# Weight casts and their checks moved from the first to the last groups of an attention stage; the raw weights stay in SBUF

## Chip, cores and metric

The kernel runs on one core of a Trainium2 chip, in one launch. The metric is the device time of that launch in microseconds (us); a run's figure is the median of its executions.

## What is computed

Four sublayers on x of shape (16, 512, 128), each of the form x = x + layernorm(f(layernorm(x))):

```python
x = x + ln(L0_attn(ln(x)))   # 16 heads of 8, keys in 8 blocks of 64, a running maximum
x = x + ln(L0_ffn(ln(x)))    # ternary weights, hidden size 512
x = x + ln(L1_attn(ln(x)))   # FFT of heads, cumulative sum, inverse FFT
x = x + ln(L1_ffn(ln(x)))    # shared expert + top-1 of 8 experts

def L0_ffn(x):
    h = silu(x @ w1.T * s1) * (x @ w2.T * s2)
    h = gelu(h @ h1.T * s_h1)
    h = gelu(h @ h2.T * s_h2)
    return h @ w3.T * s3
```

The change touches the first attention and the first MLP (L0_ffn). The weights w1, w2 (512 x 128), h1, h2 (512 x 512) and w3 (128 x 512) hold -1, 0 or 1.

## The kernel before

The program is a row of blocks, each with one hand-written stream per engine: PE (matmuls), ACT (activations, copies out of PSUM), DVE (reductions, elementwise), POOL (elementwise on SBUF), SP (all ordinary DMAs). Semaphores order them.

**The attention block** works on 16 chunks (one batch row of 512 tokens each) of 4 head groups: 64 groups g = 4 b + i. A step of the pipeline does for group g the scores and their block maxima, for g-1 the differences of maxima, for g-2 the transposed scores, exponentials and products with V, for g-3 the outputs, for g-4 the denominators. PE runs 16 scores (`score`, L568), 16 transposed scores (`score_T`, L579) and 16 products (`pv`, L589) in a step, with one use of PSUM bank 7 per quarter (`bank7`). DVE reduces each of the 16 score tiles out of PSUM (`tile_reduce`, L827), then `previous_max` (L835) ends its step; three PSUM banks rotate between PE and DVE. ACT does 16 exponentials (L678). POOL does the small work on maxima and, per chunk, three normalisations: `normed` (L775) on xnB, on y3 (then `add_residual`, L791) and on xn2. SP loads QR and KR of a group (8 DMAs of 64 KB, L479 and L481) a step ahead, two rows of maxima (`load_max`, L488), and stores q and k of a later chunk (L508, L515). `run_groups` writes steps 0 to 11 out, loops over chunks 3 to 13, and writes steps 56 to 70 out. From step 64 on no scores are left (64 groups), and DVE has only denominators, normalisations and layernorm statistics.

**Weights for the MLP.** The MLP multiplies in a rounded 32-bit type (F32R). Eleven tiles of 128 x 512 (NWB = 11: w1, w2, four of h1, four of h2, w3) are prepared inside the attention block, one per step in steps 0 to 10: SP loads tile n into one of three buffers `w_raw` (`load_weights`, L530), POOL casts it to `wb` (`cast_weights`, L796), and a step later DVE compares raw and cast (`check_weights`: L879 `not_equal` into `w_diff`, L882 `max` into `rounded`), behind `previous_max` of steps 1 to 11.

**The MLP block** starts by reducing `rounded` (L1215) to one number, and PE takes one of two written-out paths: the first multiplies with `wb` (no weight was changed by the cast), the second with 32-bit weights in buffers of its own (w1, w2, hw, w3). SP loads those five buffers (2816 KB in five DMAs, L1008 to L1012) in every run; only the second path waits for them. The trace names `wb` in all MLP matmuls (L1024): the first path runs.

## Time and profile before

| | |
|---|---|
| median of 3 runs | 1799.72 us (1798.75 to 1801.79) |
| the profiled execution's own time | 1799.19 us |
| its span, first to last instruction | 1797.3 us |
| attention block, scores of groups 0 to 63 | 46.4 to 847.7 us |
| its tail, steps 64 to 70 | 847.7 to 895.7 us |
| MLP block begins | 896 us |
| busy over the span: PE / DVE / ACT / POOL | 88% / 74% / 64% / 40% |
| mean granted clock of PE | 0.942 of full speed |

Times in the rows further down are us from the span's start unless marked ns. An arrow at a row's end names what ended the idle time before it. "PEclk" is the granted clock as a share of 2.4 GHz (0.50 is 1.2 GHz). A block of rows with one line number in it is one helper; the names left of the arrow "<-" are what is written, right of it what is read.

### The profile page before, as it was taken

To read this page: it belongs to the slowest core of one execution; us is meant where nothing else is said; L and a number is where in the kernel's file an instruction comes from. 1 tells how busy PE (TensorE), PEld (TensorE's weight loads), DVE (VectorE), ACT (ScalarE), POOL (GpSimd) and SP (SyncE) were. 2 spreads that over 40 slices of the span, in tenths; PEclk is the share of its full clock that TensorE was granted. 3 is DMA by queue.
4 is the path that set the end of the run, shared out by engine and by line. 5 is a ranking of instruction groups with operands and counts; after the bars stand their busy time and mean duration, and the time that the engine had idled before them with its cause. 6 is when DMAs were issued, how large, how long until landed. Compare 5 with 4: busy or idle time off the path is not lost. (4 is left out here: it accounts for less than half of the span.)

```text
span 1797.3 us, 35515 instructions
## 1 busy us (share of the span) xinstructions
PE 1580.2 (88%) x8576; PEld 870.8 (48%) x8577; DVE 1324.0 (74%) x3585; ACT 1146.9 (64%) x2294; POOL 713.0 (40%) x1011
## 2 busy tenths in 40 slices
PE   2899999999999999999499999999498973799996
PEld 1333333333333333333277777777345552566664
DVE  2899999999999999998257666666347763466665
ACT  1387888888888888888466666666236553344342
POOL 2223344344443333322413333333135776144444
PEclk8699999999999999999799999999799985899998
DMA  3333332232323233221010000000120112222210
GB/s 110 75 96 100 86 95 79 81 89 77 93 80 87 79 93 95 72 55 31 13 65 1 1 0 0 0 0 1 27 71 16 44 48 97 72 59 59 59 55 17
DMA packets 84446, 102.48 MB, mean 57 GB/s; under 512 B 15995, under 2 KB 49537, under 8 KB 84368
## 3 DMA queue, kind: packets, MB, share of 16 engines
q1 hardware_dynamic: 78992, 88.89, 17.6%
q0 software_dynamic: 5376, 12.66, 2.0%
q8 instruction: 35, 0.57, 0.1%
q14 instruction: 43, 0.35, 0.1%
HBM read 61.44 MB, written 35.33 MB: 54 GB/s over the span
## 5 line engine op out<-in xcount | busy, mean ns | idle before, releaser
L827 DVE TENSOR_REDUCE bmax<-PS 128x8 f32<-128x512 f32 x1024 | 651.3, 683 | 61.4 <-PE PS L568 58.8
L678 ACT ACTIVATE EX<-PS 128x512 f32<-128x512 f32 x1024 | 565.2, 604 | 107.5 <-PE PS L579 97.9
L568 PE MATMUL PS<-KR,QR 33*128 33x512 f32 x1024 | 411.2, 469 | 50.4 <-DVE bmax L827 31.3
L579 PE MATMUL PS<-QR,KR 64*128 64x512 f32 x1024 | 399.1, 460 | 1.6 <-ACT EX L678 1.5
L568 PEld LDWEIGHTS PS<-KR,QR 33*128 33x128 f32 x1024 | 167.0, 188 | 366.6 <-DVE bmax L827 299.3
L589 PE MATMUL PS<-EX,VS 128*9 128x512 f32 x2048 | 268.6, 596 | 1.2 <-ACT EX L678 1.2
L579 PEld LDWEIGHTS PS<-QR,KR 64*128 64x128 f32 x1024 | 162.5, 185 | 11.3 <-ACT EX L678 10.2
L1024 PE MATMUL PS<-pA,wb 128*128 128x512 f32 x640 | 157.0, 401 | 0.0
L763 POOL TENSOR_TENSOR m_diff<-m_prev,m_all 128x16 f32<-128x16 f32 x64 | 14.2, 222 | 328.1 <-DVE m_all L839 328.1
L1853 ACT ACTIVATE g<-PS 128x512 f32<-128x512 f32 x72 | 43.0, 597 | 142.1 <-PE PS L1813 142.1
L1024 PEld LDWEIGHTS PS<-pA,wb 128*128 128x128 f32 x640 | 120.3, 191 | 27.5
L1170 ACT ACTIVATE gelud<-PS,scales 128x512 f32<-128x512 f32 x128 | 88.3, 690 | 61.5 <-PE PS L1024 58.4
L1124 POOL CAST pA<-gated 128x512 fp32r<-128x512 f32 x64 | 57.6, 899 | 168.3 <-DVE gated L1224 167.9
L1024 PE MATMUL PS<-pB,wb 128*128 128x512 f32 x512 | 120.8, 395 | 0.0
L1024 PEld LDWEIGHTS PS<-pB,wb 128*128 128x128 f32 x512 | 96.1, 188 | 23.4
L1867 POOL TENSOR_TENSOR rs<-ve,neg_half 128x1 f32<-128x1 f32 x72 | 40.8, 566 | 131.8 <-DVE ve L1908 131.8
L1024 PE MATMUL PS<-pX,wb 128*128 128x512 f32 x256 | 75.8, 437 | 19.1 <-DVE gated L1224 16.6
L1224 DVE SCALAR_TENSOR_TENSOR gated<-PS,scales,sil 128x512 f32<-128x512 f32 x64 | 47.1, 747 | 48.2 <-ACT sil L1150 40.8
L1873 POOL DMA_INDIRECT out<-o,idx x72 | 74.4, 1033 | 17.2 <-issue 17.2
L1812 PE MATMUL PS<-sgu,xT 128*128 128x512 f32 x144 | 77.7, 621 | 0.1
L1150 ACT ACTIVATE sil<-PS,scales 128x512 f32<-128x512 f32 x64 | 43.1, 687 | 49.9 <-PE PS L1024 48.8
L1813 PE MATMUL PS<-wgu,xT 128*128 x144 | 74.4, 599 | 0.0
(227 smaller groups left out, 2821.0 us busy)
## 6 DMA issues: line engine op xcount, KB each, us to landing
QR<-q_scr SPq DMA_DIRECT2D x256, 64.0 KB, 2.4
KR<-k_scr SPq DMA_DIRECT2D x256, 64.0 KB, 2.3
k_scr<-partsB SPq DMA_DIRECT2D x42, 256.0 KB, 2.9
rows<-row_scr SPq DMA_DIRECT2D x72, 129.0 KB, 2.1
q_scr<-partsB SPq DMA_DIRECT2D x28, 256.0 KB, 3.0
X<-in_L_attn_x SPq DMA_DIRECT2D x16, 256.0 KB, 3.0
X<-x SPq DMA_DIRECT2D x16, 256.0 KB, 2.4
xB<-in_L_attn_x SPq DMA_DIRECT2D x14, 256.0 KB, 3.3
```

Source lines behind the costliest of these rows:

```text
L568: pe.matmul(PS[:, bank_of(i, n), :], QR[rows, i, h // 2, t * P:(t + 1) * P], KR[rows, i, h // 2, :], start=True, stop=True).then_inc(tile_ ...
L579: pe.matmul(PS[:, RING3 + bank_of(j, n), :], KR[rows, j, h // 2, kt * P:(kt + 1) * P], QR[rows, j, h // 2, :], start=True, stop=True).then ...
L589: mm = pe.matmul(PS[32 * h:32 * h + HD + 1, 6, :], VS[:, j, kt, h, :], EX[:, kt % 2 * HG + head_T(h), :], start=(kt == 0), stop=(kt == NT ...
L678: act.activation(EX[:, n % (2 * HG), :], PS[:, RING3 + bank_of(j, n), :], ACT.Exp, scale=SCALE).then_inc(ex_set, 1)
L827: dve.tensor_reduce(bmax[:, i % 2, n, :], PS[:, bank_of(i, n), :].rearrange("p (b k) -> p b k", k=BLK), AX_X, ALU.max).then_inc(tile_max, 1)
L1024: mm = pe.matmul(bank, lhs, rhs, start=(n == 0), stop=(n == len(todo) - 1))
L1124: pool.tensor_copy(pA[:, s, f, 0, :], gated[:, n % HR, :]).then_inc(hi0_set, 1)
L1170: act.activation(gelud[:, f, :], PS[:, f, :], ACT.Gelu, scale=scales[:, 2 + layer, f:f + 1]).then_inc(gelu_set, 1)
L1224: dve.scalar_tensor_tensor(gated[:, n % HR, :], PS[:, 2 * (n % 2) + 1, :], scales[:, 1, n % FB:n % FB + 1], sil[:, n % 2, :], ALU.mult, AL ...
L1812: pe.matmul(PS[:, 2 + 2 * s, :], xT7[:, s, 0, :], sgu[:], start=True, stop=True)
L1813: pe.matmul(PS[:, 3 + 2 * s, :], xT7[:, s, 1, :], wgu[:, ds(e * (2 * F1), 2 * F1)], start=True, stop=True).then_inc(gu7_done, 1)
L1873: pool.indirect_dma_start(out=out_rows, out_offset=bass.IndirectOffsetOnAxis(idx7[:, k:k + 1], 0), in_=o7[:, k % 4, :], in_offset=None, bo ...
```

## The change

`w_raw` becomes eleven buffers that live through the MLP. SP issues all eleven weight loads in step 56, behind the store of q. POOL waits once for all of them and casts tiles 0 to 10 in steps 57 to 62, two per step (one in step 62), at the end of its step. DVE compares tiles 0 to 10 in steps 64 to 67 (three, three, three, two), at the end of its step, and each comparison now waits for the one before. The second path of the MLP reads `w_raw`; its own buffers and their five DMAs go.

```diff
@@ -178,6 +178,7 @@
...
         NWB = 3 + 2 * (io["L0_ffn_h1_w"].shape[0] // P)
+        w_raw = sb("w_raw", [P, NWB, S], F32, mlp)
         wb = sb("wb", [P, NWB, S], F32R, mlp)
@@ -354,9 +355,8 @@
...
         ln2 = ln_bufs("ln2", p2, LN_SPLIT)
-        w_raw = sb("w_raw", [P, 3, S], F32, p2)
         w_diff = sb("w_diff", [P, S], F32, p2)
-        w_raw_in = [sem(f"w_raw_in{k}") for k in range(3)]
+        w_raw_in = sem("w_raw_in")
         w_cast = sem("w_cast")
@@ -516,9 +516,7 @@
...
                 def load_weights(n):
-                    if n >= 3:
-                        sp.wait_ge(w_checked, 2 * n - 4)
-                    dst = w_raw[:, n % 3, :]
+                    dst = w_raw[:, n, :]
                     if n < 2:
@@ -527,7 +525,7 @@
...
                         dst = dst.rearrange("p (k o) -> p k o", k=FB)
-                    sp.dma_start(dst, src).then_inc(w_raw_in[n % 3], 16)
+                    sp.dma_start(dst, src).then_inc(w_raw_in, 16)
@@ -548,8 +546,9 @@
...
                         store_x(b - 2)
-                    if isinstance(g, int) and g < NWB:
-                        load_weights(g)
+                    if isinstance(g, int) and g == ENDING * NG:
+                        for n in range(NWB):
+                            load_weights(n)
                 run_groups(sp, step, TAIL)
@@ -792,14 +791,13 @@
...
-                    pool.wait_ge(w_raw_in[n % 3], (n // 3) * 16 + 16)
-                    pool.tensor_copy(wb[:, n, :], w_raw[:, n % 3, :]).then_inc(w_cast, 1)
+                    if n == 0:
+                        pool.wait_ge(w_raw_in, NWB * 16)
+                    pool.tensor_copy(wb[:, n, :], w_raw[:, n, :]).then_inc(w_cast, 1)
...
                         maxima((i - 1) % NG, g - 1)
-                    if isinstance(g, int) and g < NWB:
-                        cast_weights(g)
                     if has(0):
@@ -815,6 +813,10 @@
...
                         low(b, i - 2)
+                    if isinstance(g, int):
+                        for n in range(NWB):
+                            if g == ENDING * NG + 1 + n // 2:
+                                cast_weights(n)
                 run_groups(pool, step, TAIL)
@@ -876,7 +878,9 @@
...
                     dve.wait_ge(w_cast, n + 1)
-                    dve.tensor_tensor(w_diff[:], w_raw[:, n % 3, :], wb[:, n, :],
+                    if n:
+                        dve.wait_ge(w_checked, 2 * n)
+                    dve.tensor_tensor(w_diff[:], w_raw[:, n, :], wb[:, n, :],
                                       ALU.not_equal).then_inc(w_checked, 1)
@@ -920,8 +924,10 @@
...
                         previous_max(i, g)
-                    if isinstance(g, int) and 1 <= g <= NWB:
-                        check_weights(g - 1)
+                    if isinstance(g, int):
+                        for n in range(NWB):
+                            if g == GROUPS + n // 3:
+                                check_weights(n)
                 run_groups(dve, step, TAIL)
@@ -936,10 +942,6 @@
...
         HR = 4
-        w1 = sb("w1", [P, DH], F32, p4)
-        w2 = sb("w2", [P, DH], F32, p4)
-        hw = [sb("h1w", [P, FB, DH], F32, p4), sb("h2w", [P, FB, DH], F32, p4)]
-        w3 = sb("w3", [P, FB, P], F32, p4)
         scales = sb("scales", [P, 4, FB], F32, p4)
@@ -953,7 +955,6 @@
...
         ln3 = ln_bufs("ln3", p4, LN_SPLIT)
-        w4_in = sem("w4_in")
         s4_in = sem("s4_in")
@@ -1005,12 +1006,6 @@
...
                 sp.dma_start(w3s[:], io["L0_ffn_w3_s"].rearrange("a o -> o a")).then_inc(s4_in, 16)
-                sp.dma_start(w1[:], io["L0_ffn_w1_w"]).then_inc(w4_in, 16)
-                sp.dma_start(w2[:], io["L0_ffn_w2_w"]).then_inc(w4_in, 16)
-                sp.dma_start(hw[0][:], io["L0_ffn_h1_w"].rearrange("(k p) o -> p k o", p=P)).then_inc(w4_in, 16)
-                sp.dma_start(hw[1][:], io["L0_ffn_h2_w"].rearrange("(k p) o -> p k o", p=P)).then_inc(w4_in, 16)
-                sp.dma_start(w3[:], io["L0_ffn_w3_w"].rearrange("(k p) o -> p k o", p=P)).then_inc(w4_in, 16)
-                sp.wait_ge(w4_in, 80)
@@ -1027,6 +1022,9 @@
...
                     return wb[:, n, f * P:(f + 1) * P]
+
+                def raw_of(n, f):
+                    return w_raw[:, n, f * P:(f + 1) * P]
@@ -1038,9 +1036,9 @@
...
                             pe.wait_ge(hi_set, 16 * p - 2 + 2 * n)
-                        for k, w in enumerate((w1, w2)):
+                        for k in range(2):
                             times(PS[:, 2 * (n % 2) + k, :],
-                                  [(w[:, f * P:(f + 1) * P], wb_of(k, f), [pX[:, s, j, :] for j in range(2)])],
+                                  [(raw_of(k, f), wb_of(k, f), [pX[:, s, j, :] for j in range(2)])],
                                   exact).then_inc(in_done, 1)
@@ -1053,7 +1051,7 @@
...
                         times(PS[:, f, :],
-                              [(hw[layer][:, k, f * P:(f + 1) * P], wb_of(2 + layer * FB + k, f),
+                              [(raw_of(2 + layer * FB + k, f), wb_of(2 + layer * FB + k, f),
                                 [src[:, s, k, j, :] for j in range(2)]) for k in range(FB)],
@@ -1062,7 +1060,7 @@
...
                     times(PS[:, 4 + s, :],
-                          [(w3[:, k, :], wb_of(NWB - 1, k), [pA[:, s, k, j, :] for j in range(2)])
+                          [(raw_of(NWB - 1, k), wb_of(NWB - 1, k), [pA[:, s, k, j, :] for j in range(2)])
                            for k in range(FB)], exact).then_inc(mlp_done, 1)
@@ -1110,7 +1108,6 @@
...
                 with pe.Else():
-                    pe.wait_ge(w4_in, 80)
                     run_pairs(pe, step_of(False))
```

The instructions move as follows. Line numbers of the changed kernel are its own: L883 and L886 are the comparison that stands at L879 and L882 before, L849 is `denominators` (L847), L854 `inverses` (L852), L862 `normalise` (L860), L871 `add_bias` (L869).

DVE before, the end of step 1 to the end of step 2:

```order
L835 TENSOR_REDUCE m_prev<-bmax 128x16
L879 TENSOR_TENSOR w_diff<-w_raw,wb 128x512
L882 TENSOR_TENSOR rounded<-rounded,w_diff 128x512
L827 TENSOR_REDUCE bmax<-PS 128x8 x2
L839 TENSOR_TENSOR m_all<-m_prev,bmax 128x16
L827 TENSOR_REDUCE bmax<-PS 128x8 x14
L835 TENSOR_REDUCE m_prev<-bmax 128x16
L879 TENSOR_TENSOR w_diff<-w_raw,wb 128x512
L882 TENSOR_TENSOR rounded<-rounded,w_diff 128x512
```

In the changed kernel steps 1 to 11 have the same rows without the two that read `w_raw` or `w_diff`.

DVE in the changed kernel, step 65 and the start of step 66:

```order
L871 TENSOR_TENSOR y3<-PS,bias 128x512
L849 SCALAR_TENSOR_TENSOR den<-corr,OTT 128x16
L123 BN_STATS lnA_st<-y3 128x6 x4
L854 RECIPROCAL rden<-den 128x16
L152 BN_AGGR lnA_mv<-lnA_st 128x2 x4
L862 TENSOR_TENSOR AOs<-OTT,rden 128x4x32
L883 TENSOR_TENSOR w_diff<-w_raw,wb 128x512
L886 TENSOR_TENSOR rounded<-rounded,w_diff 128x512
L883 TENSOR_TENSOR w_diff<-w_raw,wb 128x512
L886 TENSOR_TENSOR rounded<-rounded,w_diff 128x512
L883 TENSOR_TENSOR w_diff<-w_raw,wb 128x512
L886 TENSOR_TENSOR rounded<-rounded,w_diff 128x512
L123 BN_STATS ln2_st<-x3 128x6 x4
L849 SCALAR_TENSOR_TENSOR den<-corr,OTT 128x16
```

Six comparison instructions stand between `normalise` of step 65 and the statistics of x3 (`ln2_st`) that open step 66. Before, these two stood next to each other. Step 66 ends with six more in the same way, in front of `denominators` of step 67.

SP in the changed kernel, from `load_max` in step 56 to the start of step 57:

```order
L488 DMA QR<-m_row 2x8x128 x2
L508 DMA q_scr<-partsB 16x8x512 x2
L528 DMA w_raw<-in_L0_ffn_w1_w 128x512
L528 DMA w_raw<-in_L0_ffn_w2_w 128x512
L528 DMA w_raw<-in_L0_ffn_h1_w 128x512 x4
L528 DMA w_raw<-in_L0_ffn_h2_w 128x512 x4
L528 DMA w_raw<-in_L0_ffn_w3_w 128x4x128
L479 DMA QR<-q_scr 16x2x512
L481 DMA KR<-k_scr 16x2x512
L479 DMA QR<-q_scr 16x2x512
```

Before, the load of the next group (L479) stood right behind the store of q (L508). Eleven DMAs are now ahead of it.

## Rows read from the trace of the kernel before

**Rows 1.** Who waited for whom, 250 to 750 us (total, times, longest)

```profile
PEld PS L568 <- DVE bmax L827: 180.7, 301, 1.0
```

**Rows 2.** DVE timeline: start us, us, engine, line, op; the end of a group's reduces

```profile
148.92 0.27 DVE L835 TENSOR_REDUCE m_prev<-bmax 128x16 f32<-128x112 f32 x1
...
202.32 0.27 DVE L835 TENSOR_REDUCE m_prev<-bmax 128x16 f32<-128x112 f32 x1
...
252.93 0.27 DVE L835 TENSOR_REDUCE m_prev<-bmax 128x16 f32<-128x112 f32 x1
...
265.80 0.27 DVE L835 TENSOR_REDUCE m_prev<-bmax 128x16 f32<-128x112 f32 x1
...
302.82 0.27 DVE L835 TENSOR_REDUCE m_prev<-bmax 128x16 f32<-128x112 f32 x1
```

**Rows 3.** DVE timeline behind 202.32 (with a check) and behind 265.80 (without)

```profile
202.51 0.68 DVE L879 TENSOR_TENSOR w_diff<-w_raw,wb 128x512 f32<-128x512 f32 x1
203.23 0.69 DVE L882 TENSOR_TENSOR rounded<-rounded,w_diff 128x512 f32<-128x512 f32 x1
203.84 1.28 DVE L827 TENSOR_REDUCE bmax<-PS 128x8 f32<-128x512 f32 x2
...
266.14 1.29 DVE L827 TENSOR_REDUCE bmax<-PS 128x8 f32<-128x512 f32 x2
```

**Rows 4.** PE timeline; then stretches: us, busy by engine, PEclk, DMA share, GB/s

```profile
71.26 0.79 PE L568 MATMUL PS<-KR,QR 33*128 33x512 f32 x1 [1.01 <-DVE bmax L827]
...
77.00:78.00 1.00, 1.00 (x8) 0.47 (x4) 0.20 (x1) 0.17 (x1) 0.00 (x0) 0.50 0.00 0
...
79.00:80.00 1.00, 1.00 (x12) 0.12 (x8) 1.00 (x3) 0.82 (x4) 0.00 (x0) 1.00 0.00 0
```

**Rows 5.** Timeline of all engines, 860 to 874 us

```profile
860.75 0.26 DVE L860 TENSOR_TENSOR AOs<-OTT,rden 128x128 f32<-128x128 f32 x1
...
861.35 1.03 POOL L160 TENSOR_TENSOR lnA_rs<-lnA_ve,neg_half 128x4 f32<-128x4 f32 x1
...
862.59 3.13 POOL L775 TENSOR_SCALAR y<-y,lnA_mv,lnA_rs 128x128 f32<-128x128 f32 x4 [0.21 <-POOL lnA_rs L160]
...
867.22 0.87 DVE L123 BATCH_NORM_STATS2 ln_st<-x 128x6 f32<-128x128 f32 x4 [6.21 <-POOL x L791]
...
870.46 3.13 POOL L775 TENSOR_SCALAR xn<-x,ln_mv,ln_rs 128x128 f32<-128x128 f32 x4 [0.21 <-POOL ln_rs L160]
...
872.68 0.18 DVE L847 SCALAR_TENSOR_TENSOR den<-corr,OTT 128x16 f32<-128x16 f32 x1 [3.60 <-ACT OTT L719]
...
873.64 0.86 PE L599 MATMUL PS<-idf,xn 128*128 128x128 f32 x4 [1.61 <-POOL xn L775]
```

**Rows 6.** Three lines in the MLP (ns min/median/max), and one DVE stretch

```profile
L1124 POOL CAST pA<-gated x64: 609/905/1160, 902.6 to 1240.6; 128x512 fp32r<-128x512 f32 x64
...
L1129 POOL TENSOR_TENSOR X<-X,yv x16: 1259/1671/2172, 963.6 to 1285.4; 128x512 f32 x10, 128x512 f32<-128x512 f32 x6
...
L1229 DVE TENSOR_TENSOR pB<-gelud,pB x64: 658/686/1626, 913.2 to 1256.0; 128x512 fp32r<-128x512 f32 x64
...
1255.27 2.38 DVE L1229 TENSOR_TENSOR pB<-gelud,pB 128x512 fp32r<-128x512 f32 x2
```

**Rows 7.** SP issues and PE's next group; then DMA rates of two stretches

```profile
747.38 1.25 SPq L508 DMA_DIRECT2D q_scr<-partsB  x2
...
750.60 0.32 SPq L479 DMA_DIRECT2D QR<-q_scr  x1
...
753.76 0.42 SPq L481 DMA_DIRECT2D KR<-k_scr  x1
...
763.76 0.50 PE L568 MATMUL PS<-KR,QR 33*128 33x512 f32 x1
...
49.00:50.00 1.00, 1.00 (x3) 0.52 (x2) 1.00 (x3) 0.00 (x0) 0.00 (x0) 0.50 1.06 162
905.00:906.00 1.00, 1.00 (x4) 0.60 (x4) 1.00 (x3) 0.30 (x1) 0.88 (x1) 1.00 1.01 365
```

## Prediction

> **What bounds the kernel now.** I read the page's list of costliest lines first (DVE's score reductions, ACT's exponentials and PE's scores all run through the attention block), then the waits of a steady stretch, then the DVE timeline group by group, and last the timeline of the block's tail, where the change puts work. The waits say what limits a steady group: PE's weight loads for the next score stood 180.7 us out of 500 behind DVE's reduction of a tile, 301 times and never over 1 us [rows 1]. So PE and DVE run hand in hand over three PSUM banks, and DVE is mostly the one waited for. A DVE instruction added to a group should therefore show in the group's length, though not at full price.
>
> It does. `previous_max` (L835) closes each group on DVE. Groups 8 to 11, each with one weight check in it, took 202.32 - 148.92 = 53.40 us; groups 16 to 19, with the same other work and no check, took 302.82 - 252.93 = 49.89 us [rows 2]. **That is 3.51 us for four checks, 0.88 us each.** On DVE itself a check is two instructions of 0.68 and 0.69 us; from `previous_max` to the next reduction it is 203.84 - 202.32 = 1.52 us with them and 266.14 - 265.80 = 0.34 us without [rows 2, 3], so 1.18 us of engine time, of which PE's own pace hides a quarter.
>
> The tail, steps 64 to 70, is another regime. No scores are left, all engines are mostly idle, and one chain sets the end: POOL normalises y3 of chunk 14, adds the residual, DVE takes the statistics of x3, POOL normalises xn2, PE transposes it, and only then is bank 7 free for the last chunk. In rows: `y` from 862.59 (3.13 us), the statistics at 867.22 after 6.21 us in which DVE waited for POOL, `xn` from 870.46 (3.13 us), and PE at 873.64, 1.61 us idle until POOL's `xn` came [rows 5]. There POOL is late, not DVE.
>
> **The change, part by part.**
>
> *Eleven checks leave steps 1 to 11.* The check behind group g lengthens group g + 1, so ten lie in groups 3 to 12, and I price each at the measured 0.88 us: 8.8 us. The first is in group 2, where PE is still at half clock: PE stood 1.01 us for DVE's reduction at 71.26, and from there it works without idling until the granted clock goes from 0.50 (1.2 GHz, 77 to 78 us) to 1.00 (2.4 GHz, 79 to 80 us) [rows 4]. Taking that 1.01 us away lets PE do 1.01 us of half-clock work earlier, worth about half at full clock: 0.5 us. **Together -9.3 us.** Bounds: if only the measured groups and group 12 count in full and the lighter chunk 1 (no `add_bias`, no statistics of y3 and x3) hides half of its share, 3.5 + 0.9 + 1.8 = 6.2 us; if all eleven count with both instructions at full length, 11 x 1.37 = 15.1 us. I stay with 0.88, the only like-for-like difference in the trace.
>
> *Eleven casts go from steps 0 to 10 to steps 57 to 62 on POOL.* Each is about 0.61 us there as a cast alone (the shortest cast of this size takes 609 ns [rows 6]), two in a row 1.2 us, placed at the end of POOL's step. POOL then waits several us for the next group's maxima, which hides them. What can show is a small DVE instruction that reads two SBUF tiles (`denominators`) meeting a cast: at most 0.6 us in three of the six steps, and DVE gets back the same meetings from the old place. I put +0.3 us (0 to 1.8).
>
> *Eleven loads go to step 56 in one burst.* SP is free after the store of q, at 747.38 + 1.25 = 748.6. Its issues are (753.76 - 750.60) / 7 = 0.45 us apart [rows 7], so eleven take 5.0 us and the load of group 57 (eight DMAs) starts at 753.6 instead of 750.60, ending its issue near 757.2. The bytes ahead of PE's next group are 0.5 MB of q, 2.9 MB of weights, 0.5 MB of QR and KR: 3.9 MB. At the 365 GB/s that the same weights reach in the MLP they take 10.7 us and are in at about 759.3, and PE starts group 57 at 763.76 [rows 7]. Behind them only the two small rows of maxima follow. 4 us of cover: 0 us. Casts wait for all eleven loads, but come a whole group later. At the start the missing loads were waited for by nobody but POOL, so nothing is gained there.
>
> *Five loads leave the MLP block.* They are issued behind the five small scale loads that ACT waits for, and only the path that does not run waits for them: 0 us. The names in the MLP's matmuls change only on that path.
>
> *Eleven checks arrive in steps 64 to 67.* Those of steps 64 and 67 meet a DVE that waits for PE and a POOL that waits for DVE: free. Six instructions start when `normalise` of step 65 is done, at 860.75 + 0.26 = 861.0, and need 6 x 0.7 = 4.2 us, up to 865.3; DVE's next work is at 867.22. On DVE they fit. In step 66 they start near 869.1 and end near 873.3, 0.6 us behind `den` at 872.68 [rows 5]; but PE first transposes `xn` (873.64), and the result of `den` is needed after that, so this costs nothing either. What does not fit is **what they do to POOL**. Each is an instruction with two SBUF inputs, and both sets lie exactly over POOL's critical chain (861.35 to 865.7, and again to 873.6). In the MLP such instructions run beside POOL: its cast takes 905 ns in the median against 609 at least, its residual addition 1671 against 1259, and a pair of DVE instructions that should take 1.37 took 2.38 us [rows 6]. So a POOL instruction that meets a DVE one loses 0.3 to 0.4 us there, and sometimes it is DVE that loses. In each of the two steps POOL has a `pow` and four pieces of 0.78 us. I charge 0.2 for `pow`, and 0.5 for each of four pieces (between the 0.41 of the median and 0.69, a whole DVE instruction, since here DVE has the next one ready each time): 2.2 us per step. **Two steps, +4.4 us**, one for one on the chain. Bounds: if POOL keeps its turn once it has begun, only the first meeting costs, 0.3 + 0.3 per step, +1.2 us; if each of the twelve instructions holds POOL up for its whole 0.69 us, +8.3 us.
>
> The Trainium skill (SBUF — State Buffer, "Who interferes with whom") speaks against this placement: a DVE instruction with two SBUF inputs and a GpSimd instruction that reads SBUF do not share, the second to come is blocked until the first has finished. The 2.38 us agrees. Strictly alternating, every one of POOL's eight pieces would wait up to a whole DVE instruction, 8 x 0.69 + 0.4 = 5.9 us, and the sum would be 1.5 us worse than mine.
>
> **Sum:** -9.3 + 0.3 + 4.4 = -4.6 us. The profiled execution took 1799.19 us, so 1794.6; the median of the runs is 0.5 higher, so I say 1795.0.
>
> **The rivals.**
>
> *A, the tail costs little.* POOL keeps its turn and DVE waits instead: -9.3 + 0.3 + 1.2 = -7.8, 1791.7 us. For it: DVE instructions were seen to wait too (2.38 us). Against it: half of all casts in the MLP took 905 ns or more. With more of the 1.18 us per check coming back it reaches 1790.
>
> *B, little comes back.* The lighter groups of chunk 1 are bound by PE, 6.2 us early, and the tail costs 5.9: 1799.7 + 0.3 - 6.2 + 5.9 = 1799.7 us, no change. For it: a quarter of a check is hidden already in heavy groups. Against it: the 3.51 us of rows 2 were found with PE's work in place, and the tail would have to cost its strict price as well.
>
> *C, PE's clock rises earlier.* With the 1.01 us gap at 71.26 closed [rows 4], PE's unbroken stretch begins some 2 us earlier. If the rise comes 2 to 3 us sooner, 1 to 1.5 us more are won: about 1793.5 us. Nothing shows that it would move.
>
> *D, the burst stops PE: slower.* If the weights come in at the rate of the mixed stretch at the start, 162 GB/s with all DMA engines busy [rows 7], 3.9 MB take 24 us and group 57 is complete at 772.7, 8.9 us after 763.76; with the tail at +4.4 that is 1799.7 - 4.6 + 8.9 = 1804.0 us. It decides below 3.9 MB / 15.2 us = 257 GB/s. Against it: that stretch moved short pieces beside few large ones, and the large weights alone ran at 365.
>
> *E, the change does not do what it says.* If the cast weights were not what the first path reads, nothing would move; but the same `wb` and `rounded` are filled and tested, so I give it nothing.
>
> **How the numbers follow.** Chances: the forecast 0.45, A 0.21, B 0.17, C 0.07, D 0.10. 0.2% is 3.6 us, about what a measurement of this kernel can tell from no change. The forecast lies 4.7 below the median, so of its 0.45 some 0.35 is faster by more than that and 0.10 is not; A and C are faster (0.28), D slower (0.09 of its 0.10), and B leaves 0.15 within, 0.01 slower and 0.01 faster. Faster 0.64, within 0.26, slower 0.10. The range goes from A with the better early price (1789.5) to B with a little of D (1800.5); what is left out is the rest of D and the ends of the bounds.
>
> **What would show it.** Right: `previous_max` to `previous_max` for groups 8 to 11 at 49.9 us; PE idle before 71.26 gone; group 57 starting without a wait for a DMA; POOL's `y` and `xn` in steps 65 and 66 at 5 us each instead of 3.13, and PE's transposition of `xn` 4 to 5 us later against the end of group 63. Wrong: those two still at 3.1 to 3.5 us (A), groups 8 to 11 still above 51.5 us (B), PE waiting for KR or QR in group 57 (D).

## Result and the profile after

| | before | after |
|---|---|---|
| median of 5 runs, one chip | 1798.75 us (1797.83 to 1801.79) | 1789.77 us (1787.0 to 1792.4) |
| ratio of the times | | 0.9947, 95% interval 0.9934 to 0.9960 |
| profiled execution | 1799.19 us | 1791.91 us |
| its span | 1797.3 us | 1790.1 us |
| `previous_max` of group 12 | 215.90 us | 204.15 us |
| `previous_max` of group 63 | 847.67 us | 836.40 us |
| PE starts the first transposition of `xn` in the tail | 873.64 us | 864.85 us |
| first matmul of the MLP | 898.20 us | 889.70 us |

The change makes the kernel 9.0 us faster (0.53%, interval 0.40 to 0.66%). The forecast was 4.7 us. The direction and the range were right, the size was not: about half of the gain was not foreseen.

First the early groups. DVE timeline of the kernel after, the ends of groups 7, 11 and 12 (start us, us, engine, line, op); L837 is `previous_max`:

```profile
141.54 0.27 DVE L837 TENSOR_REDUCE m_prev<-bmax 128x16 f32<-128x112 f32 x1
...
191.20 0.27 DVE L837 TENSOR_REDUCE m_prev<-bmax 128x16 f32<-128x112 f32 x1
...
204.15 0.27 DVE L837 TENSOR_REDUCE m_prev<-bmax 128x16 f32<-128x112 f32 x1
```

From the end of group 7 to the end of group 11 it is 191.20 - 141.54 = 49.66 us where it was 53.40 [rows 2], and 49.9 had been forecast. The lead of the new kernel over the old grows by 9.24 us from the end of group 2 to the end of group 12 and then stays: 11.75 us at group 12, 11.69 at group 56. A steady group is as it was. The waits say the same; of 250 to 740 us after (total, times, longest):

```profile
PEld PS L567 <- DVE bmax L829: 177.2, 296, 1.0
```

Over the same 490 us of the kernel before it was 176.2 us, 294 times, so the balance of PE and DVE has not moved. PE's own waits in groups 3 to 12 have. The first fence is of the kernel before, 85 to 216 us, the second of the one after, 82 to 205 us:

```profile
PE PS L568 <- DVE bmax L827: 9.2, 19, 0.9
```

```profile
PE PS L567 <- DVE bmax L829: 4.1, 10, 0.6
```

With a comparison behind each group, PE stood nineteen times, up to 0.9 us; now it is ten times and never over 0.6. In group 2, PE no longer stands 1.01 us [rows 4], and in this profile the granted clock rises sooner. Stretches of the kernel after (us, busy of PE, PEld, DVE, ACT, POOL, then PEclk, DMA share, GB/s):

```profile
74.00:75.00 1.00, 1.00 (x6) 0.32 (x4) 0.00 (x0) 0.00 (x0) 0.31 (x1) 0.50 0.00 0
75.00:76.00 1.00, 1.00 (x7) 0.41 (x5) 0.48 (x1) 0.45 (x1) 0.00 (x0) 0.80 0.00 0
76.00:77.00 1.00, 1.00 (x8) 0.36 (x12) 1.00 (x3) 0.82 (x4) 0.00 (x0) 1.00 0.00 0
```

The rise from 1.2 to 2.4 GHz lies at 75.4 us, 18.5 us behind the end of group 0; in the first profile of the kernel before it was 20.7 us behind.

Now the burst. SP issues and PE's next group in the kernel after (the unit "SPq" is SP's own queue of issues), then two stretches:

```profile
736.03 1.30 SPq L508 DMA_DIRECT2D q_scr<-partsB  x2
737.38 1.11 SPq L528 DMA_DIRECT2D w_raw<-in_L_ffn_w_w  x2
738.53 4.21 SPq L528 DMA_DIRECT2D w_raw<-in_L_ffn_h_w  x8
...
743.35 0.43 SPq L479 DMA_DIRECT2D QR<-q_scr  x1
...
752.12 0.18 PEld L567 LDWEIGHTS PS<-KR,QR 33*128 33x128 f32 x1 [0.17 <-DMA KR<-k_scr]
...
752.13 0.50 PE L567 MATMUL PS<-KR,QR 33*128 33x512 f32 x1
```

```profile
744.00:746.00 2.00, 2.00 (x15) 0.58 (x7) 1.81 (x5) 1.47 (x4) 0.00 (x0) 1.00 1.03 387
...
748.00:750.00 2.00, 2.00 (x18) 0.83 (x16) 2.00 (x4) 2.00 (x5) 0.00 (x0) 1.00 0.97 159
```

The matmuls do not stand here, but PE's weight load waits 0.17 us for KR. The last of the eight loads of QR and KR landed at 752.08 us, 0.05 us before PE began group 57; in the kernel before it landed at 756.27, 7.5 us before 763.76 [rows 7]. The DMA engines are busy without a pause from 738 to beyond 752 us, and between 748 and 750 us, when the bytes of the weights are through and the eight 64 KB loads of QR and KR (16 partitions each) are left, the rate is 159 GB/s. Groups 56 to 63 cost 0.40 us of the lead.

Last the tail. The kernel before, where it begins with `add_bias` of step 65, and POOL's two smaller steps that [rows 5] leave out:

```profile
858.60 0.69 DVE L869 TENSOR_TENSOR y<-PS,bias 128x512 f32<-128x512 f32 x1 [9.72 <-PE PS L604]
...
861.03 0.19 POOL L158 TENSOR_SCALAR lnA_ve<-lnA_mv 128x4 f32<-128x4 f32 x1 [12.07 <-DVE lnA_mv L152]
...
869.22 1.03 POOL L160 TENSOR_TENSOR ln_rs<-ln_ve,neg_half 128x4 f32<-128x4 f32 x1
```

The timeline of POOL, DVE and PE in the kernel after (L883 and L886 are the comparison; L160 is `pow`):

```profile
847.32 0.69 DVE L871 TENSOR_TENSOR y<-PS,bias 128x512 f32<-128x512 f32 x1 [5.32 <-PE PS L603]
...
849.65 0.68 DVE L883 TENSOR_TENSOR w_diff<-w_raw,wb 128x512 f32<-128x512 f32 x1
849.75 0.63 POOL L158 TENSOR_SCALAR lnA_ve<-lnA_mv 128x4 f32<-128x4 f32 x1 [12.06 <-DVE lnA_mv L152]
...
850.47 1.48 POOL L160 TENSOR_TENSOR lnA_rs<-lnA_ve,neg_half 128x4 f32<-128x4 f32 x1
...
852.15 3.90 POOL L774 TENSOR_SCALAR y<-y,lnA_mv,lnA_rs 128x128 f32<-128x128 f32 x4 [0.21 <-POOL lnA_rs L160]
...
857.55 0.87 DVE L123 BATCH_NORM_STATS2 ln_st<-x 128x6 f32<-128x128 f32 x4 [2.94 <-POOL x L790]
...
859.54 1.35 POOL L160 TENSOR_TENSOR ln_rs<-ln_ve,neg_half 128x4 f32<-128x4 f32 x1
...
861.11 3.69 POOL L774 TENSOR_SCALAR xn<-x,ln_mv,ln_rs 128x128 f32<-128x128 f32 x4 [0.21 <-POOL ln_rs L160]
...
864.85 1.11 PE L598 MATMUL PS<-idf,xn 128*128 128x128 f32 x4 [3.98 <-POOL xn L774]
```

POOL is slower wherever a comparison lies over it. Against the kernel before, `lnA_ve` went from 0.19 to 0.63 us, `pow` from 1.03 to 1.48 and 1.35, `y` from 3.13 to 3.90, `xn` from 3.13 to 3.69. From `add_bias` of step 65 to PE's transposition of `xn` it is 17.53 us against 15.04: +2.49 us.

### The profile page after: what moved, and what is told of

Its sections match the earlier page's. It is cut to its first block and busy times, and to the rows that moved or that the text cites. A ratio compares the mean times of both kernels' runs of the same rounds, so it can differ in the third digit from the quotient of the medians.

```text
span 1790.1 us, 35518 instructions
## 1 busy us (share of the span) xinstructions
PE 1578.8 (88%) x8576; PEld 871.7 (49%) x8577; DVE 1326.2 (74%) x3585; ACT 1146.3 (64%) x2294; POOL 714.8 (40%) x1011
## 5 line engine op out<-in xcount | busy, mean ns | idle before, releaser
L567 PE MATMUL PS<-KR,QR 33*128 33x512 f32 x1024 | 408.2, 468 | 43.6 <-DVE bmax L829 24.5
L1019 PE MATMUL PS<-pX,wb 128*128 128x512 f32 x256 | 77.7, 447 | 18.6 <-DVE gated L1221 16.6
L1870 POOL DMA_INDIRECT out<-o,idx x72 | 74.5, 1035 | 17.6 <-issue 17.6
```

What stands on the lines that cost most here:

```text
L567: pe.matmul(PS[:, bank_of(i, n), :], QR[rows, i, h // 2, t * P:(t + 1) * P], KR[rows, i, h // 2, :], start=True, stop=True).then_inc(tile_ ...
L1019: mm = pe.matmul(bank, lhs, rhs, start=(n == 0), stop=(n == len(todo) - 1))
L1870: pool.indirect_dma_start(out=out_rows, out_offset=bass.IndirectOffsetOnAxis(idx7[:, k:k + 1], 0), in_=o7[:, k % 4, :], in_offset=None, bo ...
```

## The experiments

Each profile is measured between the same places (`previous_max` of a group is its end). "g0 to g2" and "g2 to g12" are the lead over the first profile of the kernel before that is won between the ends of those groups (negative is sooner), "loss 56-63" what is lost again from group 55 to 63, "tail" the 15.04 us stretch above, "rise" the time from the end of group 0 to the rise of the clock, all in us.

| profile | g0 to g2 | g2 to g12 | loss 56-63 | tail | rise |
|---|---|---|---|---|---|
| before | 0 | 0 | 0 | 15.04 | 20.7 |
| before, second (e7) | -0.77 | -0.06 | 0.01 | 15.04 | 18.4 |
| before, third (e12) | -0.17 | +2.11 | -0.02 | 15.12 | 20.3 |
| before, fourth (e13) | +2.99 | +3.43 | -0.03 | 15.08 | 36.5 |
| before, fifth (e14) | -0.73 | -0.08 | -0.05 | 15.04 | 18.6 |
| e9, first comparison out | -2.18 | +1.45 | -0.03 | 15.57 | 16.8 |
| after | -1.43 | -9.24 | 0.40 | 17.53 | 18.5 |
| after, second (e8) | -1.96 | -9.23 | 0.51 | 17.52 | 17.3 |
| e1, no comparisons | -2.10 | -9.21 | 0.91 | 15.04 | 17.0 |
| e2, one-input | -2.24 | -9.21 | 0.52 | 15.03 | 16.7 |
| e3, only comparisons late | -2.10 | -9.24 | -0.04 | 17.55 | 17.0 |
| e4, loads from step 2 | -2.08 | -9.23 | 0.01 | 17.54 | 17.0 |
| e5, comparisons in gaps | -1.42 | -9.21 | 3.20 | 15.50 | 18.6 |
| e6, longer burst | -1.77 | -9.21 | 6.69 | 17.53 | 17.6 |
| e10, e3 and e5 together | -1.41 | -9.29 | 0.00 | 15.54 | 18.5 |
| e11, e10 again | -1.96 | -9.26 | 0.00 | 15.41 | 17.3 |

### e1: the comparisons left out

```diff
                             if g == GROUPS + n // 3:
-                                check_weights(n)
+                                pass
```

> The changed kernel with the eleven comparisons of steps 64 to 67 left out (the flag that they fill stays zero, so the comparison of raw and cast weights isn't made). In the changed kernel PE's transposition of xn comes 17.53 us after DVE's y of step 65 (847.32 to 864.85), before it was 15.04 us (858.60 to 873.64). Theory P (the comparisons hold up POOL): this falls back to 15.0 us and POOL's y and xn stretches to 3.13 us each, and the whole launch is about 2.7 us shorter than the changed kernel's. Rival Q (the tail is longer for another reason, such as the new place of the buffers in SBUF): it stays near 17.5 us. The early groups keep the changed kernel's lengths in both.

Measured: 1787.66 us (1786.49 to 1788.13) against 1799.84, ratio 0.9928 (0.9904 to 0.9952). The tail is 15.04 us again. So the comparisons cost the tail 2.49 us, and nothing else that the change does lengthens it. PE's matmuls did wait for the burst here; PE timeline of e1 behind the store of q:

```profile
752.95 0.50 PE L567 MATMUL PS<-KR,QR 33*128 33x512 f32 x1 [0.48 <-DMA KR<-k_scr]
```

### e2: the same number of DVE instructions, each with one SBUF input

```diff
-                    dve.tensor_tensor(w_diff[:], w_raw[:, n, :], wb[:, n, :],
-                                      ALU.not_equal).then_inc(w_checked, 1)
+                    dve.tensor_reduce(w_diff[:, 0:1], w_raw[:, n, :], AX_X, ALU.max).then_inc(w_checked, 1)
                     dve.wait_ge(w_checked, 2 * n + 1)
-                    dve.tensor_tensor(rounded[:], rounded[:], w_diff[:], ALU.max).then_inc(w_checked, 1)
+                    dve.tensor_reduce(w_diff[:, 1:2], w_raw[:, n, :], AX_X, ALU.max).then_inc(w_checked, 1)
```

> The changed kernel with each comparison instruction of steps 64 to 67 replaced by a reduction of the same 128x512 tile with one SBUF input (no comparison is made). DVE stays as busy as with the comparisons, about 0.69 us per instruction. Theory P1 (what holds POOL up is the second SBUF input of the comparison): POOL's y and xn stretches are back at 3.13 us and y of step 65 to the transposition of xn is 15.0 us. Rival P2 (what costs is that DVE is busy when its own next instruction comes, or any DVE access to SBUF): it stays near 17.5 us, with POOL's stretches at 3.7 to 3.9 us.

Measured: 1787.59 us (1783.94 to 1788.92), ratio 0.9929 (0.9905 to 0.9954). Timeline of POOL, DVE and PE in e2's tail:

```profile
849.06 0.68 DVE L883 TENSOR_REDUCE w_diff<-w_raw 128x1 f32<-128x512 f32 x1
849.17 0.20 POOL L158 TENSOR_SCALAR lnA_ve<-lnA_mv 128x4 f32<-128x4 f32 x1 [12.06 <-DVE lnA_mv L152]
849.45 1.03 POOL L160 TENSOR_TENSOR lnA_rs<-lnA_ve,neg_half 128x4 f32<-128x4 f32 x1
...
850.69 3.14 POOL L774 TENSOR_SCALAR y<-y,lnA_mv,lnA_rs 128x128 f32<-128x128 f32 x4 [0.21 <-POOL lnA_rs L160]
851.29 0.69 DVE L885 TENSOR_REDUCE w_diff<-w_raw 128x1 f32<-128x512 f32 x1
...
858.58 3.14 POOL L774 TENSOR_SCALAR xn<-x,ln_mv,ln_rs 128x128 f32<-128x128 f32 x4 [0.21 <-POOL ln_rs L160]
...
861.77 0.66 PE L598 MATMUL PS<-idf,xn 128*128 128x128 f32 x4 [1.63 <-POOL xn L774]
```

DVE is as busy in the same places, each instruction takes the same 0.68 or 0.69 us, and POOL keeps its 0.20, 1.03, 3.14 and 3.14 us. So it is not DVE's work as such that held POOL up. But e2 takes away two things, the second SBUF input and the output of 512 elements (its reductions write one per partition). The profile of the kernel before separates them. In its MLP, `gate` (L1224) reads one tile from PSUM and one from SBUF and writes 512 elements, and L1229 reads two tiles from SBUF and writes as many; each meets POOL's cast of the same size:

```profile
957.05 0.68 DVE L1229 TENSOR_TENSOR pA<-gated,pA 128x512 fp32r<-128x512 f32 x1
957.30 0.91 POOL L1124 CAST pA<-gated 128x512 fp32r<-128x512 f32 x1 [0.36 <-DVE gated L1224]
...
1040.09 0.74 DVE L1224 SCALAR_TENSOR_TENSOR gated<-PS,scales,sil 128x512 f32<-128x512 f32 x1
1040.35 0.61 POOL L1124 CAST pA<-gated 128x512 fp32r<-128x512 f32 x1 [14.14 <-DVE gated L1224]
```

The eight casts that meet only L1224 took 0.61 us each, the seventeen that meet only L1229 took 0.90 us or more. The output of 512 elements costs POOL nothing; the second SBUF input is what held it up.

### e3: only the comparisons late; e4: loads from step 2

e3 puts loads and casts back into steps 0 to 10, with their waits, and leaves the comparisons in the tail (main lines of the edit; the late casts go as well):

```diff
-                    if isinstance(g, int) and g == ENDING * NG:
-                        for n in range(NWB):
-                            load_weights(n)
+                    if isinstance(g, int) and g < NWB:
+                        load_weights(g)
...
                         maxima((i - 1) % NG, g - 1)
+                    if isinstance(g, int) and g < NWB:
+                        cast_weights(g)
```

> The changed kernel with only the DVE comparisons moved: loads and casts of the eleven tiles are back in steps 0 to 10 (eleven raw buffers stay). The changed kernel was ahead of the one before by 1.08 us at the end of group 0, by 1.43 us more at the end of group 2 and by 9.24 us more by group 12 (11.75 in all). Theory S (the 1.08 us of group 0 come from the missing weight loads, which ran beside the loads of groups 0 and 1; all the rest from DVE's comparisons): group 0 ends at 58.0 us as before, and the lead by group 12 is 10.2 to 11 us. Rival R (group 0's lead is chance of the execution or comes from the buffers' places): group 0 ends at 56.9 us here too. Rival C (casts on POOL cost DVE time as well): the lead in groups 3 to 12 is under 8.5 us.

e4 is the same, but tiles 0 to 2 are loaded together in step 2 and cast, with tile 3, in step 3 (main lines):

```diff
-                    if isinstance(g, int) and g == ENDING * NG:
-                        for n in range(NWB):
+                    if isinstance(g, int) and 2 <= g < NWB:
+                        for n in ((0, 1, 2) if g == 2 else (g,)):
                             load_weights(n)
...
+                    if isinstance(g, int) and 3 <= g < NWB:
+                        for n in ((0, 1, 2, 3) if g == 3 else (g,)):
+                            cast_weights(n)
```

> As e3, but tiles 0 to 2 are loaded in step 2 and cast in step 3, so that steps 0 and 1 have no weight load. Theory S: group 0 ends at 56.9 us, 1.1 us ahead of e3, and that lead is kept to group 12. Rival R: no difference between the two in group 0. PE's clock: if the rise from 0.50 to 1.00 comes with PE's own progress, it is at 75 to 76 us here and in the changed kernel and 76 to 78 in e3; if it is chance, the three differ by up to 3 us without order.

Measured: e3 1790.40 us (1788.99 to 1792.02), ratio 0.9948 (0.9924 to 0.9971); e4 1788.37 us (1785.71 to 1789.55), ratio 0.9928 (0.9902 to 0.9954). With all loads and casts back among the first groups, e3 wins the whole 9.24 us of groups 3 to 12 and as much in group 2 as any other. **The early gain is the comparisons' alone**; moving loads and casts won nothing. Nor do the first two loads delay group 0: it ended at 58.33 us in e3 and 57.39 in e4, but at 57.34 to 59.65 in the five profiles of the kernel before. What both gain is that groups 56 to 63 lose nothing, since there is no burst.

### e5: comparisons where POOL does not read SBUF

Seven tiles in step 64, four in step 67, none in steps 65 and 66, with two `w_diff` buffers, so that one tile's `max` runs behind the next tile's `not_equal` (`check_tiles` issues them in that order):

```diff
                     if isinstance(g, int):
-                        for n in range(NWB):
-                            if g == GROUPS + n // 3:
-                                check_weights(n)
+                        if g == GROUPS:
+                            check_tiles(list(range(7)))
+                        if g == GROUPS + 3:
+                            check_tiles(list(range(7, NWB)))
```

> The changed kernel with the comparisons where POOL is idle: seven tiles in step 64 and four in step 67, none in steps 65 and 66, with two difference buffers so that a comparison need not wait for the one before. Theory P1 (two SBUF inputs of DVE against POOL's reads): fourteen instructions of 0.6 us fit in the 9.8 us before DVE's y of step 65, eight in the 5.7 us before the last y, so y of step 65 to the transposition of xn is 15.0 us as without comparisons, POOL's stretches are 3.13 us, and the attention block ends 2.5 to 2.8 us earlier than in the changed kernel against group 63. Rival Q2 (DVE's work in step 64 or 67 is itself late for y): y of step 65 comes more than 11.0 us after the end of group 63, or the last y is later, and up to 2 us of it are lost again.

Measured: 1788.02 us (1786.3 to 1791.1) against 1799.88, ratio 0.9940 (0.9924 to 0.9957). The tail is 15.50 us: 2.0 of the 2.49 us come back, and `add_bias` of step 65 is as soon behind group 63 as before (10.92 us). What stays, 0.46 us, is mostly 0.42 us that DVE stood without a reason that the profile shows; it is in the three profiles of this arrangement and, with 0.37 us, in e9, which has no comparison there, so whether they cause it stays open. In this execution the burst cost more than it had in any before; PE timeline of e5:

```profile
756.15 0.50 PE L567 MATMUL PS<-KR,QR 33*128 33x512 f32 x1 [1.88 <-DMA KR<-k_scr]
```

After it the granted clock fell to 0.50 for some 3 us: 3.20 us lost in all.

### e6: a longer burst

Eight more DMAs of 256 KB, from DRAM to DRAM, stand behind the eleven, and the casts wait for all nineteen:

```diff
                             load_weights(n)
+                        for n in range(8):
+                            sp.dma_start(again[n], io[("L0_ffn_h1_w", "L0_ffn_h2_w")[n // FB]]
+                                         [n % FB * P:(n % FB + 1) * P]).then_inc(w_raw_in, 16)
```

> The changed kernel with eight more DMAs of 256 KB (weights copied within DRAM) behind the eleven of step 56. In the run without comparisons PE stood 0.48 us for a KR load in group 57; in the changed kernel it stood for none. Theory B (the burst is at the edge of what hides: group 57's QR and KR stand behind it in SP's queue and on the DMA engines): eight more issues (3.7 us) and 2 MB put group 57 behind by 3 to 8 us, seen as PE waiting for KR or QR and as a longer distance from the end of group 56 to that of 57. Rival (the loads of a group overtake the burst, and 0.48 us was jitter): group 57 is less than 1 us longer.

Measured: 1796.5 us (1795.28 to 1800.33, 10 runs), against 1799.88, ratio 0.9989 (0.9978 to 0.9999). SP and PE timelines of e6:

```profile
744.16 5.07 SPq L554 DMA_DIRECT2D again<-in_L_ffn_h_w  x8
749.35 0.50 SPq L480 DMA_DIRECT2D QR<-q_scr  x1
...
757.96 0.79 PE L571 MATMUL PS<-KR,QR 33*128 33x512 f32 x1 [4.91 <-DMA KR<-k_scr]
```

The load of group 57 is issued at 749.35 instead of 743.35, 6.0 us later, and PE stands 4.91 us, then works at half clock: 6.69 us lost, most of what the change had won. So hardly anything of the 4 us of cover was there: 6.0 us more of issues and 2 MB more gave 4.9 us of wait.

### e7, e12, e13, e14: the kernel before, unedited

> The kernel before once more, for a second profile of it. If PE's clock rises in group 2 by chance of the execution, its time scatters over 3 us here too (it was between 78 and 79 us, against 73 to 76 us in the five runs without early comparisons); if the gap behind the first comparison sets it, it is between 78 and 79 again, counted from the end of group 0 20.4 us. In the MLP the clock rose 2.9 us after the first matmul; the three runs with comparisons in steps 65 and 66 had it 7.6 to 8.3 us after.

> The kernel before, unedited, for a third profile. PE's clock rose 20.7 and 18.4 us after the end of group 0 in two profiles with the first comparison in place, and 16.7 to 18.6 in eleven profiles without it. Theory (closing the gap in front of PE in group 2 brings the rise forward): this profile and the next two rise at 18.4 or later, with a mean of 19 to 20 us. Rival (the rise only scatters from one execution to the next): they spread over 16.7 to 18.6 like the others. In the MLP the rise comes 3 to 4 or 7 to 10 us after the first matmul, in either kernel.

> The kernel before, unedited, a fourth profile: as for the third. Theory: the rise comes 18.4 us after the end of group 0 or later. Rival: 16.7 to 18.6. The lengths that no clock changes stay as they are: groups 2 to 12 at 0.0 within 0.1, y to the transposition of xn 15.04 (or 0.45 more where the gap of issue before the statistics' aggregate shows, as in the run without the first comparison).

> The kernel before, unedited, a fifth profile: as for the third. Theory: the rise comes 18.4 us after the end of group 0 or later. Rival: 16.7 to 18.6. With it the lead of group 2 over five profiles of the unchanged kernel gives what the early part won there: 1.4 to 2.2 us against the first profile, so 0.5 to 1.5 against their mean by the theory, and 0 to 0.5 at the same clock.

Measured: e7 1799.93 us (1796.73 to 1803.72), ratio 1.0007 (0.9995 to 1.0019). The other three are one execution each, on another chip: 1806.09, 1811.66 and 1801.52 us, beside 1804.85 for one more of the same kernel. Their rises are in the table, none under 18.4 us. The expectation that groups 2 to 12 stay within 0.1 us failed in e12 and e13: these two show what the first two profiles had not, a clock that falls again among the first groups. Stretches of e12 at the start of group 9, and of e13 in group 5:

```profile
165.00:166.00 1.00, 0.50 (x2) 0.19 (x2) 1.00 (x4) 0.95 (x3) 0.20 (x2) 1.00 0.27 78
166.00:167.00 1.00, 0.54 (x4) 0.42 (x4) 1.00 (x3) 0.24 (x1) 0.92 (x5) 1.00 0.50 131
167.00:168.00 1.00, 1.00 (x9) 0.42 (x12) 1.00 (x5) 0.87 (x2) 0.28 (x2) 0.89 0.21 66
168.00:169.00 1.00, 1.00 (x8) 0.00 (x0) 1.00 (x5) 0.70 (x2) 0.00 (x0) 0.50 0.00 0
```

```profile
117.00:118.00 1.00, 0.74 (x6) 0.19 (x2) 0.96 (x3) 0.81 (x3) 0.00 (x0) 1.00 0.67 184
118.00:119.00 1.00, 0.34 (x2) 0.19 (x2) 1.00 (x3) 0.46 (x1) 0.00 (x0) 0.94 0.54 152
119.00:120.00 1.00, 1.00 (x6) 0.71 (x4) 1.00 (x4) 0.60 (x1) 0.53 (x3) 0.50 0.50 148
```

PE is busy half of the time while DVE is busy nearly without a pause: these are PE's waits of 0.9 us for a DVE that has just done a comparison. Behind them the clock goes from 2.4 to 1.2 GHz. In e12 group 9 took 16.15 us instead of 13.94, in e13 group 5 took 13.82 instead of 12.41 (and group 3 14.89 instead of 12.85, since the clock had not yet risen).

### e9: the first comparison left out

```diff
-                    if isinstance(g, int) and 1 <= g <= NWB:
+                    if isinstance(g, int) and 2 <= g <= NWB:
                         check_weights(g - 1)
```

> The kernel before with one edit: the comparison behind step 1 (tile 0) is left out, so its gap of 1.01 us in front of PE in group 2 goes, and the other ten comparisons stay. Left out of the computation: whether the cast changed tile 0. Theory: the end of group 2 comes 0.5 to 0.8 us sooner against the end of group 0 where the clock rises 18.4 us after it (as in the second profile of the kernel before, so 1.3 to 1.6 against the first), and groups 2 to 12 are as before (0.0 within 0.1); time 1799.3. Rival (forecast's case C: closing the gap brings the clock's rise 2 to 3 us forward): rise at 17.7 or less after group 0 and group 2 shorter by 2 us against the first profile, time 1798.

Measured: 1797.75 us (1796.7 to 1803.19) against 1797.01, ratio 1.0008 (0.9996 to 1.0019): no difference. The expectation of 1799.3 us by its theory and 1798 by its rival can't be told apart by that time. The rise comes 16.8 us after group 0 and group 2 ends 2.18 us sooner than in the first profile, as case C had it. Then the gain is lost in the next group, where the second comparison stands. Stretches of e9:

```profile
83.00:84.00 1.00, 0.51 (x6) 0.18 (x2) 0.96 (x3) 0.85 (x2) 0.00 (x0) 1.00 0.57 141
84.00:85.00 1.00, 0.56 (x2) 0.18 (x2) 1.00 (x4) 0.24 (x1) 0.00 (x0) 0.82 0.40 117
85.00:86.00 1.00, 1.00 (x3) 0.50 (x2) 1.00 (x3) 0.60 (x1) 0.76 (x4) 0.50 0.42 125
```

And PE's wait in the second of them:

```profile
84.44 0.64 PE L568 MATMUL PS<-KR,QR 33*128 33x512 f32 x1 [0.93 <-DVE bmax L827]
```

### e8: the kernel after, again; e10 and e11: early loads and casts, comparisons in the gaps

e10 and e11 are one kernel, the edits of e3 and e5 together.

> The changed kernel once more, with nothing edited, for a second profile and more times. In the first profile of it PE's clock rose 18.5 us after the end of group 0 and, in the MLP, 8.3 us after the first matmul; groups 56 to 63 lost 0.40 us beside the burst; the tail (y of step 65 to the transposition of xn) took 17.53 us. Theory (the tail is set by instructions, the clock and the burst by the execution): tail 17.5 again within 0.05, groups 2 to 12 at -9.2 again, while the clock's two rises differ by a us or more from the first profile and the loss beside the burst is anywhere from 0 to 1 us. Rival (the change itself makes the clock rise late in the MLP): 8 us or more again. Time 1789.8 within 1.5.

> Loads and casts of the tiles in steps 0 to 10 as before (where they cost DVE and PE nothing: 11.3 us lead from group 0 to group 12, as without them), comparisons in the gaps of steps 64 and 67. Expected by the theories so far: lead over the kernel before of 11.3 us from the end of group 0 to group 12, none of it lost in groups 56 to 63 (0.4 to 0.9 us were, with the burst and late casts), tail 15.0 us; the attention block 11 us shorter than before. If the burst and the late casts are harmless, it equals the run with the burst and comparisons in the gaps.

> e10 again (loads and casts in steps 0 to 10, comparisons in the tail, placed into DVE's idle time of steps 64 to 67 and in pairs over two buffers), with more rounds, beside the changed kernel on one chip. By the stages of its profile it should win 2.0 us in the tail and 0.4 in groups 56 to 63 over the changed kernel: 2.4 us, 1787.4 where the changed kernel takes 1789.8. Theory: its median is 1 to 3 us below e8's in the same batch. Rival (what the tail and the burst cost is lost in the scatter between executions): within 1 us of it.

Measured: e10 1789.17 us (1784.42 to 1791.37) against 1799.88, ratio 0.9954 (0.9937 to 0.9971). Side by side on one chip, before 1797.01 us: e8 1789.89 us (1788.29 to 1791.92), ratio 0.9961 (0.9947 to 0.9976); e11 1788.27 us (1784.51 to 1789.76), ratio 0.9951 (0.9937 to 0.9965). e8 repeats the first profile's tail (17.52) and groups 3 to 12 (9.23), and loses 0.51 us beside the burst; the clock's rise in the MLP comes 4.2 us behind the first matmul, not 8.3, so its lateness was the execution's. DVE and POOL in e11's tail:

```profile
848.10 0.87 DVE L123 BATCH_NORM_STATS2 lnA_st<-y 128x6 f32<-128x128 f32 x4 [0.42 <-issue]
...
851.26 3.13 POOL L775 TENSOR_SCALAR y<-y,lnA_mv,lnA_rs 128x128 f32<-128x128 f32 x4 [0.21 <-POOL lnA_rs L160]
...
859.13 3.13 POOL L775 TENSOR_SCALAR xn<-x,ln_mv,ln_rs 128x128 f32<-128x128 f32 x4 [0.21 <-POOL ln_rs L160]
```

POOL has its 3.13 us back and groups 56 to 63 lose nothing: 2.1 and 0.5 us less than e8 by the stages. The medians differ by 1.6 us in that direction, but their intervals overlap, so this is the better arrangement by its profile and not shown to be by its time.

## Why the prediction was wrong

**Ten comparisons at 0.88 us: right.** 8.8 us was forecast for groups 3 to 12, 9.24 us came, 0.92 each, the same within 0.08 us in all ten profiles of kernels without early comparisons. That is 0.4 us more than forecast. The bound of 6.2 us (chunk 1 hides half) and rival B fall with it: the light groups pay in full.

**Group 2 at 0.5 us: this step failed.** I priced one PE gap and gave the clock's earlier rise a rival of its own at 0.07. The instruction part is 0.66 us: at equal rise (18.4 to 18.6 us) two profiles of before stand at -0.77 and -0.73, and three without the comparison at -1.41 to -1.43. On top of that come two effects of the clock. First the rise: five profiles of the kernel before have it 18.4 to 36.5 us behind group 0, median 20.3; the eleven without the first comparison have 16.7 to 18.6, median 17.3. A rise 1.5 us sooner (17.0 for 18.5) is worth 0.67 us (2.10 for 1.43), and in the kernel before 2.2 us are worth 0.75, so 3 us are worth an estimated 1.0 to 1.3. These are counts of executions, and the two sets of rises meet at 18.4 to 18.6 us. Second the falls, which no case of mine had: of six profiles with comparisons behind groups 2 to 11, three (e9, e12, e13) lost 1.4 to 2.2 us to a clock that fell behind PE's 0.9 us waits; of the ten without them, none. From the end of group 0 to that of group 12 the median lead of those ten is 11.2 us over the first profile, which is the median of the five of before. I had 9.3. That is 1.9 us of the miss: 0.4 in the ten comparisons and 1.5 in group 2, which won 1.96 us in the median of the ten where I had 0.5. The falls are not in this figure, since the first profile had none; where one comes, the kernel before is that much slower still. That the clock fell for PE's waits is an inference from the order of events and these counts. It fits that in e5 and e6, with no comparison in those groups, the clock also fell behind PE waits, of 1.88 and 4.91 us for a DMA; it did not behind the 0.48 us in e1.

**The tail at +4.4 us: this step failed too**, in size and not in kind. It cost 2.49 us. The terms, before against after: in step 65 `lnA_ve` 0.19 to 0.63, `pow` 1.03 to 1.48, `y` 3.13 to 3.90, together 1.66; in step 66 `pow` +0.32, `xn` +0.56, together 0.88. I had charged 0.5 for each of eight pieces, 4.0 us; the two stretches of four lost 0.77 and 0.56. I took the 0.5 from the MLP's cast and residual addition, which move 512 elements in one instruction, and applied it to pieces of 128 elements that follow one another closely; and I had nothing for `lnA_ve`, which met the first comparison at its start and lost 0.44. The comparisons lost little in turn, up to 0.82 us for 0.69 in steps 65 and 66. e2 and the MLP's casts show the cause, the second SBUF input. The rule of the Trainium skill (SBUF — State Buffer, "Who interferes with whom") is borne out in its condition, two inputs against one, but read as strict alternation it gave 5.9 us, more than twice what came. 1.9 us of the miss lie here, so this is case A in part: it had 1.2 us, 2.5 were measured.

**The comparisons of steps 64 and 67 free, `den` in step 66 free: right.** `add_bias` of step 65 is 10.92 us behind group 63 in every profile, 10.93 before, and e1 and e2 show nothing beyond the 2.49 us.

**The burst with 4 us of cover, 0 us: near, and only by luck.** The sum of bytes at 365 GB/s put the end 4.5 us ahead of PE. It was 0.05 us ahead in the profile after, and PE's matmuls waited 0.20 us in e8, 0.48 in e1 and 1.88 in e5. From the issue of q's store to the last landing the forecast had 759.3 - 747.38 = 11.9 us; it took 752.08 - 736.03 = 16.05, a mean of 243 GB/s for the 3.9 MB. The step that failed is the rate: 290 to 387 GB/s while the weights come in (2 us stretches from 738 to 748 us), and 159 GB/s for the loads of QR and KR behind them (748 to 750 us). That is case D's mechanism at a small price: group 57 took 13.01 us in the profile after, 13.11 in its second and 13.53 in e1, where it was 12.87 before, and 15.79 in e5, where the clock fell as well.

**Casts +0.3 us: right.** Of the 0.40 us lost in groups 56 to 63, 0.24 are in step 60, where `denominators` took 0.54 us instead of 0.18 beside two casts (0.53 in e8), and 0.14 in group 57, beside the burst. **Five MLP loads gone, 0 us: nothing speaks against it.** The MLP block took 395.24 us against 393.88. The difference goes with the granted clock, in all sixteen profiles. After its rise it falls to 0.50 again for short stretches in every MLP, five times in some executions and six in others. With a rise 8.0 to 8.8 us behind the first matmul and six falls the block took 395.1 to 395.3 us (after, e3 to e6, and the unchanged kernel in e13). With a rise at 3.0 to 4.2 and six falls it took 393.8 to 394.2 (before, e1, e2, e8, e11, e12), and with a rise at 9.2 to 9.5 and five falls 393.6 to 394.0 (e7, e14, e9). The one with an early rise and five falls, e10, took 392.3. So by these profiles a late rise costs some 1.3 us and one more fall 1.1 to 1.9 us, in kernels of either kind, and nothing is left for the change itself.

**The sum by measured terms:** -11.2 early, +2.5 in the tail, +0.4 to 0.5 beside the burst and the casts, -8.3 us. Two comparisons of the whole change gave -9.0 and -7.1 us (1797.01 to 1789.89), and it lies between them. The two profiled executions differ by 7.3 us: -1.1 for a group 0 that ended sooner (it scatters by more in the unchanged kernel), -10.7 early, +0.4 and +2.5, +0.3 in the rest of the tail, +1.4 in the MLP, -0.1 behind it. The rest of the launch after the MLP scatters by more than any term here but the first. And it does not scatter alike: the six profiles with comparisons in the early groups have 505.2 to 509.2 us there, the first one of the kernel after has 505.1, and the nine others 501.7 to 503.0. In four of the five profiles of the unchanged kernel (not e7) the last four chunks of the router in the last block took 28.7 to 31.4 us, in all twelve others 24.5 to 24.9. If some of that comes with the change, it is a gain that neither the forecast nor the sum has. No run separates it. My errors of 1.9 us in the early groups and 1.9 in the tail had the same sign, and so the forecast came out at half. One small slip besides: case A's own terms give 1799.7 - 7.8 = 1791.9 us, not 1791.7.

## What to carry to other kernels

Price an instruction on the engine that the tensor engine waits for by the length of the group, with and without it, and then ask what its gaps do to the clock: in three executions of six here the clock fell behind such gaps, at 1.4 to 2.2 us each, so take several profiles of the kernel before. Off the critical engine, put DVE work with two SBUF inputs where GpSimd is idle, not merely where DVE is. And for a burst of loads, add up to the landing of the last load that is queued behind it, and price those small loads at the rate that such loads reach, not at that of the burst.

## What the runs showed of the hardware that was not expected

- The granted clock fell from 1.00 to 0.50 in the middle of dense work, behind two stretches in which PE was about half busy (0.50 and 0.54, 0.51 and 0.56, 0.74 and 0.34 of a us), in three executions of the six with comparisons in the early groups (one of a kernel with the first left out, two of the unchanged kernel) and not in the other three.
- The rise at the start came 36.5 us behind group 0 in one execution of the kernel before, 18.4 in another; in the first PE was busy in every us from 75 to 94 us, at 0.50 throughout. Why it rose no sooner, the profile doesn't show.
- A one-input DVE reduction over 128 x 512 elements beside GpSimd's normalisation costs neither anything (3.14 us for 3.13, 0.69 for 0.69); one with two SBUF inputs, of the same 0.69 us, adds 0.44 to an instruction of 0.19 us and 0.45 to one of 1.03 us that handle 4 elements per partition.
- With the DMA engines at a share of 1.0 throughout, the rate was 387 GB/s while 256 KB weight tiles of 128 partitions were in the queue and 159 GB/s 4 us later, when loads of 64 KB into 16 partitions were left. Why they are slower, no run shows.
